# Attention block on one core: the reciprocals of the softmax sums move from VectorE to GpSimd

## The reference

```python
x = L0_attn_x                                    # 8 x 1024 tokens of 256 numbers, f32
q, k, v = (split_heads(_tlin(x, w, s, b)) for each)      # 16 heads of 16; _tlin: x @ w.T * s + b
scores = jnp.einsum('bhqd,bhkd->bhqk', q, k) / jnp.sqrt(jnp.float32(HEAD))
attn = jax.nn.softmax(scores, axis=-1)
ctx = jnp.einsum('bhqk,bhkd->bhqd', attn, v)
x = _layernorm(x + _tlin(ctx, w_o, s_o, b_o))
x = _layernorm(x + fp4_linear(silu(fp4_linear(x, w_gate)) * fp4_linear(x, w_up), w_down))
```

## Time and profile before

| what | value |
|---|---|
| runs | 1978.06, 1971.41, 1972.64 us |
| median of the runs | 1972.64 us |
| the profiled execution | 1978.5 us, its span 1976.7 us |
| busy in the span: PE, DVE, ACT, POOL | 1921.4, 1846.1, 1639.0, 749.1 us |
| share of DVE and of PE in the chain that ended last | 64%, 31% |
| mean granted TensorE clock | 0.997 of full speed |

### The profile page before, as it was taken

The page is one execution under the profiler, slowest core; times in us unless marked ns, Lnnn a source line. Parts: engine busy times, 40 slices in busy tenths (PEclk is TensorE's granted clock), DMA queues, the critical chain, the costliest instruction groups (busy, mean ns, idle before and its releaser), DMA issues.

```text
span 1976.7 us, 43274 instructions
## 1 busy us (share of the span) xinstructions
PE 1921.4 (97%) x15934; PEld 1130.0 (57%) x15934; DVE 1846.1 (93%) x3237; ACT 1639.0 (83%) x3225; POOL 749.1 (38%) x747
## 2 busy tenths in 40 slices
PE   8999999999999999999999999999999999999998
PEld 7767444444444444444444444444478888888876
DVE  4798999999999999999999999999289999999997
ACT  5555889889898998989899898988967777777776
POOL 3000455666674362010001001000046666666785
PEclk9999999999999999999999999999999999999999
DMA  7985643354445435444543544452011111111210
GB/s 219 287 241 218 124 63 52 62 106 93 86 90 102 94 72 108 91 87 89 104 94 72 103 95 88 88 104 93 24 49 49 49 49 49 50 50 55 62 33 28
DMA packets 127200, 181.48 MB, mean 92 GB/s; under 512 B 37836, under 2 KB 82636, under 8 KB 126988
## 3 DMA queue, kind: packets, MB, share of 16 engines
q1 hardware_dynamic: 119308, 171.10, 37.3%
q10 hardware_dynamic: 7392, 7.34, 1.2%
q0 software_dynamic: 288, 0.27, 0.1%
HBM read 103.68 MB, written 73.40 MB: 90 GB/s over the span
## 4 chain that ended last, share of the span: by engine, by line
DVE 64%; PE 31%; issue 3%; DMA 1%; ACT 1%; SPq 0%; DVEq 0%; POOLq 0%; POOL 0%; ACTq 0%
DVE halfmax L1135 50%; PE ps L1401 11%; DVE halfmax L1130 7%; PE ps L1440 6%; PE ps L493 4%; PE ps L1389 2%; PE ps L505 2%; PE ps L1412 2%; PE ps L1045 1%; PE ps L1011 1%; PE ps L1448 1%; PE ps L480 1%; DVE room L1591 1%; PE ps L1457 1%; DVE room L1678 1%
## 5 line engine op out<-in xcount | busy, mean ns | idle before, releaser
L1096 ACT ACTIVATE room<-ps 128x512 f32<-128x512 f32 x2048 | 1085.0, 601 | 123.3 <-PE ps L1011 101.5
L1135 DVE TENSOR_REDUCE halfmax<-ps 128x1 f32<-128x512 f32 x1714 | 1040.3, 680 | 0.1
L1011 PE MATMUL ps<-qs,ks 50*128 50x512 f32 x2048 | 715.9, 448 | 2.4 <-DVE halfmax L1135 1.3
L986 PE MATMUL ps<-ks,qs 48*128 48x512 f32 x1960 | 667.0, 436 | 23.8 <-DVE halfmax L1130 22.4
L1045 PE MATMUL ps<-room,vals 128*17 128x256 f32 (+2 forms) x8192 | 578.2, 384 | 0.3 <-ACT craw L1104 0.3
L986 PEld LDWEIGHTS ps<-ks,qs 48*128 48x128 f32 x1960 | 314.2, 184 | 423.4 <-DVE halfmax L1135 308.1
L164 POOL CAST mrow<-turned_rows 128x32 fp32r<-128x32 f32 x32 | 6.7, 209 | 896.4 <-DVE turned_rows L159 688.5
L1011 PEld LDWEIGHTS ps<-qs,ks 50*128 50x128 f32 x2048 | 326.6, 184 | 22.8 <-ACT room L1096 14.5
L1045 PEld LDWEIGHTS ps<-room,vals 128*17 128x17 f32 x8192 | 167.3, 96 | 232.4 <-issue 167.6
L1401 PE MATMUL ps<-wguT,xqT 128*128 128x512 f32 (+1 forms) x1152 | 268.3, 386 | 3.9 <-DVE xqT L1631 3.9
L1401 PEld LDWEIGHTS ps<-wguT,xqT 128*128 128x128 f32 x1152 | 211.9, 189 | 51.8 <-issue 9.9
(11 more groups left out here) (119 smaller groups left out, 2202.1 us busy)
## 6 DMA issues: line engine op xcount, KB each, us to landing
qk_parts<-parts SPq DMA_DIRECT2D x64, 512.0 KB, 4.0
qs<-qk_parts SPq DMA_DIRECT2D x192, 128.0 KB, 4.4
ks<-qk_parts SPq DMA_DIRECT2D x192, 128.0 KB, 7.0
ctx_raw<-craw SPq DMA_DIRECT2D x64, 256.0 KB
ready<-passing SPq DMA_DIRECT2D x27, 512.0 KB, 6.2
pairs<-ready SPq DMA_DIRECT2D x27, 512.0 KB
out_dram<-fin SPq DMA_DIRECT2D x64, 128.0 KB, 2.1
xin<-in_L_attn_x_dram ACTq DMA_DIRECT2D x14, 512.0 KB, 5.6
```

The source lines that it names most:

```text
L986: nc.tensor.matmul(ps[:, MX + max_number(i, u, bank) % 4, :], qs[rows, i.slot(RING), pair, t * P:(t + 1) * P], ks[rows, i.slot(RING), pair ...
L1011: nc.tensor.matmul(ps[:, score_bank(i, s, n), :], ks[rows, slot, pair, kt * P:(kt + 1) * P], qs[rows, slot, pair, qh * BANK:(qh + 1) * BAN ...
L1096: nc.scalar.activation(prob[:, prob_slot(i, s), score_order(i, s)[n], :], ps[:, score_bank(i, s, n), :], ACT.Exp, scale=float(D) ** -0.5). ...
L1135: nc.vector.tensor_reduce(halfmax[:, i.slot(2), bank, column:column + 1], ps[:, at + bank, :], AX.X, ALU.max, negate=True).then_inc(max_re ...
```

## The change

`numbers` gets a fifth column with -1.0. In `attend`, DVE no longer calls `invert_sums`. POOL gets `invert`, a power of `sums` with that column as the exponent, and calls it ahead of `part` in each `next_maxima` from group 2 on, there for group g - 2, and once more for group 30 after its last call. The reciprocals of group 31 stay on DVE, in `feed`.

```diff
-        numbers = sb("numbers", [P, 4])
+        numbers = sb("numbers", [P, 5])
...
-        for n, value in enumerate((EPS, -0.5, 1e-12, FLAT)):
+        for n, value in enumerate((EPS, -0.5, 1e-12, FLAT, -1.0)):
...
-        pool.wait_ge(numbers_ready, 4)
+        pool.wait_ge(numbers_ready, 5)
...
-                if s == 4 and i.plus(-1).ok(NGR):
-                    invert_sums(nc, dve, i.plus(-1), sums, craw_stored, rden_ready)
...
+        def invert(i):
+
+
+            for qh in range(QH):
+                pool.wait_ge(craw_stored[qh], i.lin(32, 32))
+            nc.gpsimd.tensor_tensor(sums[:, :, :], sums[:, :, :],
+                                    numbers[:, 4:5].unsqueeze(2).to_broadcast([P, QH, BANK // SB]),
+                                    ALU.pow).then_inc(rden_ready, 1)
+
         def next_maxima():
 
 
+            if group[0] >= 2:
+                invert(At(None, group[0] - 2, RING))
             maxima_out.part(nc, pool, At(None, group[0], RING))
             group[0] += 1
...
         while group[0] < NGR:
             next_maxima()
+        invert(At(None, NGR - 2, RING))
```

## The result

The changed kernel takes 1993.8 us in the median of six runs (1993.07 to 1996.55), the kernel before 1975.65 us in six (1971.41 to 1978.06), three of them measured beside it. The ratio is 1.0097, with a 95% interval of 1.0084 to 1.0111: **slower by 19 us**, where 6.9 us less were forecast. The time lies inside the range of 1963 to 2000 us, in the case "the loop becomes the bound", which had 0.30. It lies there by the width of the range: with the measured length of the power (5.43 us) the prediction's own steps give a loss of about 16.6 us (14 at 5, 20 at 6) and, less 7.8, a kernel that is 9 us slower, not 19.

The account below looks back on a forecast made before the run. The prediction took DVE alone to bound `attend`: 7.8 us less from 30 reciprocals, 0.9 us lost in the loop, -6.9 us in sum, so 1972.6 us becomes 1966 us, range 1963 to 2000.

Parts of the forecast that it names:

- the loop becomes the bound: Rival, chance 0.30: power above 5 us, PE's first score tiles of groups 7 to 10 held; 1999 us at T = 8.
- DVE is the bound of `attend`, and PE could run faster: In `attend`, DVE alone is the chain; PE's own group is about 36 us against 38.5, so DVE's savings shorten groups.
- DVE gives up time that isn't returned: Rival, chance 0.05: PE is as slow as DVE in `attend`, so the time stays at 1972.6 us.
- its place in the chain is 0.26 us: Each reciprocal leaving DVE in `attend` saves 0.26 us; 30 of them make 7.8 us less.
- I take T = 2.2 us: Length T of POOL's power of 32 columns, taken as 2.2 us between ends of 0.63 and 12.4.
- The loop and its place: SP waits for POOL's power behind the weight steps, POOL for SP's loads: laps of 37.7 + T in iterations 6 to 9.
- 5.9 us with the gaps: SP's part of a lap: `store_rden`, the store of `passing`, the next half's store and the loads, 5.9 us.
- 4T - 7.9: Loss from four late laps: 4 x (T - 0.85) - 4.5 us, nothing up to T = 2, 0.9 us at T = 2.2.
- At the end free up to T = 5: Group 30's power stands ahead of the powers of `feed` on POOL and costs nothing up to T = 5 us.

Follow-up runs that it names:

- copy: The changed kernel with the power replaced by a GpSimd copy of the sums onto themselves, inversions left out: ratio 0.9982 to the kernel before.
- early: The changed kernel with the power behind the fifth of eight weight steps instead of behind all: ratio 0.9985, 1971.66 us against 1975.34 for the kernel before.
- two: The kernel before with a second reciprocal of the same tile on DVE in each group, into an unused tile: ratio 1.0028, groups 38.70 us apart.
- moved: The kernel before with DVE's reciprocal two steps later, between two single maxima instead of right behind a pair: ratio 1.001, groups 38.59 us apart.
- half: The changed kernel with the power over only the first 16 of 32 columns, the rest left uninverted: ratio 1.0041, 8 us above the kernel before.
- late: The changed kernel with DVE inverting groups 0 to 15 and GpSimd only 16 to 30, where it has no weight steps: ratio 0.999 to the kernel before.
- six: The changed kernel with six weight steps an iteration instead of eight: ratio 0.9987, 1971.35 us against 1974.34 for the kernel before.
- ahead: The changed kernel with SP's store of `passing` issued ahead of its wait for the reciprocals: ratio 1.0081, some 16 us above the kernel before.
- double: The changed kernel with the power made twice, first into an unused tile: ratio 1.0353, 70 us above the kernel before.
- swap: The changed kernel with SP's DMAs of the maxima issued ahead of the loads into `passing`: ratio 1.0222, 45 us above the kernel before.

## Why the prediction was wrong, point by point

- *DVE is the bound of `attend`, and PE could run faster:* right in the main; wherever the reciprocal has left DVE and PE doesn't wait for the maxima, the groups are shorter (38.39 against 38.50 us). At one place of each group it is not so. The rival "DVE gives up time that isn't returned", with 0.05, came true there for 0.1 us of the 0.20.
- *"its place in the chain is 0.26 us", so 30 x 0.26 = 7.8 us:* **failed.** It is 0.11 us a group and 3.1 us in all (`copy`, `early`). 0.05 of the 0.26 came back already, because the second maximum behind a reciprocal starts sooner (0.20 exposed, `two` and `moved`), and 0.1 was hidden by PE. I had compared PE's mean pace with DVE's, and not the one place at which the reciprocal stood.
- *"I take T = 2.2 us":* **failed**, 5.43 us. This is the step that turned the sign: up to T = 2 the formula has no loss. The range of 0.63 to 12.4 us held it. The rate of add and subtraction says nothing of a power: it costs 0.157 us a column, where they cost 0.002. The rate of the Trainium skill (GPSIMD Engine Reference, section 3.1), about 2.6 cycles an element, holds for those and not for the power. Its advice to keep elementwise work on DVE is right here for the length of the instruction, 5.43 against 0.34 us for the reciprocal; for the program `early` is against it, with the power on GpSimd and the time below that of the kernel before.
- *The loop and its place:* right. PE waits at the first score tile of groups 7, 9 and 10, in `half` of 8, 9 and 10, where groups 7 to 10 were named, and the waits are gone where the power leaves the iterations with weight steps (`late`), where these have fewer steps (`six`), and where the power stands further ahead among them (`early`). It is the mechanism of the rival that happened.
- *"5.9 us with the gaps" for SP:* **mis-sized**, 7.0 us. I had added durations of issues that stood apart in time. Pushed together, they show the waits for landings between them (`ahead`).
- *4T - 7.9 as the whole loss:* with SP's part mended it gives about PE's waits in `half`, but for the longer waits it leaves out the **clock**, which the prediction put at nothing without a word: 9.0 of the 21.3 us here. The lap also gains from it: the long group 7 let GpSimd catch up, so that group 8 waited for next to nothing, and PE's waits sum to 12.3 us and not to the 16.6 that the steps give for T = 5.43, or the 18.2 of the formula with SP's part at 7.0 us.
- *At the end free up to T = 5:* free at 5.43 too. The last power ends at 1421.0 us and the first of `feed` starts at 1421.9.
- The sum with measured terms: -3.1 + 12.3 + 9.0 = +18.2 us, against 18.1 in the traces and a ratio of 1.0097. The 9.0 is a remainder, so the sum has to close. Against the 9 us that the steps give with the right T, 4.7 are DVE's gain, 9.0 the clock, and -4.3 the waits.

## What to carry to other kernels

An instruction that is moved to an engine with idle time takes its successors' waits along: ask where in that engine's order it stands, what signal it gives, and who is queued behind that signal, then add up the closed lap and compare it with the period. A lap that is longer by a few us costs nothing for some rounds and then all of it. A shorter lap cures it (`six`, `copy`), but the place of the instruction in the order can do it alone (`early`). Before a saving on the bound engine is counted in full, look at that very place for the second engine: here its lead over the first, bank by bank, was all that could be given back.

## What was unexpected of the hardware

- GpSimd's power costs 0.41 us and 0.157 us a column of 128 f32: 0.57, 2.91 and 5.43 us for 1, 16 and 32 columns. A copy of 32 columns takes 0.21 us.
- The length of a short wait of PE doesn't tell what the clock does. Gaps of its score tiles that were longer than usual by 1.2 and 1.8 us (`half`) left the clock at 1.00, but one longer by 1.7 us in `double` (at 842.46 us) was followed by 6.8 us at 0.50, and one longer by 1.6 us in `swap` (at 817.75) by 3.4 us. All that were longer by 2.2 to 11.0 us were followed by stretches at 0.50. In the changed kernel and in `half` such a wait cost 1.4 to 2.5 times its length (6.14 us for 4.3, 8.7 for 3.5).
- The busy time of DVE, whose instructions overlap, hides waits of up to 0.1 us: it shows 199.99 us of 200 in the kernel before, although behind the first pair of each group, where no reciprocal stands, its maxima are 0.68 us apart once, and not 0.60.
